# Expert loop of an attention and mixture-of-experts kernel: the high halves turned by transposing transfers, the low halves turned by TensorE as 2-byte blocks, 71 tiles instead of 72

## The reference

```
def _L0_ffn_ref(x, gate_w, expert_w):
    scores = jnp.einsum('bsh,eh->bse', x, gate_w)
    chosen = jnp.argmax(scores, axis=-1)
    onehot = jax.nn.one_hot(chosen, gate_w.shape[0], dtype=x.dtype)
    expert_out = jnp.einsum('bsh,efh->bsef', x, expert_w)
    return x + jnp.einsum('bsef,bse->bsf', expert_out, onehot)
x = x + _L0_xattn_ref(_layernorm(x, axis=-1), ctx_512, ctx_512, ...)
x = x + _L0_ffn_ref(_layernorm(x, axis=-1), L0_ffn_gate_w, L0_ffn_expert_w)
```

## Time and profile before

| | us |
|---|---|
| median of three runs | 975.7 |
| the profiled execution | 974.3 |
| its span, first to last instruction | 972.2 |
| PE busy in the span | 905.9 |
| DVE busy | 779.4 |
| POOL busy | 530.6 |
| ACT busy | 556.4 |
| PE, DVE, ACT and POOL busy between 760 and 960 us | 200.0, 119.0, 39.4, 145.4 |

### The profile page before, as it was taken

The page is one execution under the profiler, slowest core; times in us unless marked ns, Lnnn a source line. Parts: engine busy times, 40 slices in busy tenths (PEclk is TensorE's granted clock), DMA queues, the critical chain, the costliest instruction groups (busy, mean ns, idle before and its releaser), DMA issues. The chain is left out here.

```text
span 972.2 us, 27544 instructions
## 1 busy us (share of the span) xinstructions
PE 905.9 (93%) x8838; PEld 546.2 (56%) x8839; DVE 779.4 (80%) x1812; ACT 556.4 (57%) x928; POOL 530.6 (55%) x565
## 2 busy tenths in 40 slices
PE   5999999999899999899999999999775999999995
PEld 3446666556565665566556566566643555555552
DVE  8997999989699998879999889887793555555553
ACT  4686867768578686676867768657631111111110
POOL 2425454654546546455564554635552777777774
PEclk9998999999999999999999999998887999999998
DMA  9323142443424425233342542229233555555550
GB/s 316 98 69 108 39 138 75 135 124 75 134 62 138 120 72 150 68 122 102 97 143 59 146 106 65 78 67 327 77 131 98 169 170 172 163 167 167 174 174 21
DMA packets 81447, 119.51 MB, mean 123 GB/s; under 512 B 20465, under 2 KB 45797, under 8 KB 81327
## 3 DMA queue, kind: packets, MB, share of 16 engines
q1 hardware_dynamic: 68207, 81.63, 31.1%
q0 software_dynamic: 12048, 36.28, 9.9%
q10 hardware_dynamic: 1072, 0.02, 0.1%
HBM read 55.24 MB, written 38.13 MB: 96 GB/s over the span
## 5 line engine op out<-in xcount | busy, mean ns | idle before, releaser
L535 POOL TENSOR_TENSOR p_lo<-pf,p_hi 77x512 f16<-77x512 f32 x128 | 148.1, 1162 | 210.5 <-ACT p_hi L1128 210.2
L1127 ACT ACTIVATE pf<-scoresT,exp_scale 77x512 f32<-77x512 f32 x256 | 174.4, 681 | 73.2 <-PE scoresT L860 60.7
L1630 PE MATMUL mo<-e_w,x2T_hi 128*128 x576 | 184.5, 382 | 0.7 <-DVE x2T_lo L1667 0.7
L1128 ACT ACTIVATE p_hi<-scoresT,exp_scale 77x512 f16<-77x512 f32 x256 | 174.8, 683 | 0.0
L1650 ACT ACTIVATE x2T_hi<-mt 128x512 f16<-128x512 f32 x72 | 43.0, 597 | 183.4 <-PE mt L1619 183.4
L1677 DVE SCALAR_TENSOR_TENSOR res<-mo,inv,row 128x512 f32<-128x512 f32 x72 | 54.1, 751 | 91.6 <-PE mo L1630 91.6
L535 DVE TENSOR_TENSOR p_lo<-pf,p_hi 77x512 f16<-77x512 f32 x128 | 103.2, 822 | 14.8 <-ACT p_hi L1128 13.4
L1215 DVE TENSOR_REDUCE negmax<-work 128x4 f32<-128x308 f32 x256 | 112.6, 468 | 0.3 <-PE work L912 0.3
L1630 PE MATMUL mo<-e_w,x2T_lo 128*128 x288 | 110.1, 382 | 0.0
L1601 POOL DMA_INDIRECT out<-res,row x72 | 71.5, 993 | 65.4 <-DVE xn L1662 57.1
L832 PE MATMUL work<-wo_hi,cT_hi 128*128 128x512 f16 x256 | 97.3, 380 | 0.7 <-DVE cT_lo L1193 0.6
(11 more groups left out here) (257 smaller groups left out, 2179.5 us busy)
## 6 DMA issues: line engine op xcount, KB each, us to landing
row<-rows_by_expert SPq DMA_DIRECT2D x72, 257.5 KB, 3.0
q_st<-q_hi SPq DMA_DIRECT2D x256, 64.0 KB, 2.0
xt<-in_x SPq DMA_DIRECT2D x15, 1024.0 KB, 7.4
q_st<-q_lo SPq DMA_DIRECT2D x128, 64.0 KB, 2.0
ebuf<-in_L_ffn_expert_w SPq DMA_DIRECT2D x14, 512.0 KB, 8.3
er<-in_L_ffn_expert_w SPq DMA_DIRECT2D x7, 1024.0 KB, 14.9
out<-res,row POOLq DMA_INDIRECT x72, 2.8
xt<-in_x SPq DMA_DIRECT2D x4, 256.0 KB, 6.2
```

The costliest lines, as they stand in the source:

```text
L535: return tt.tensor_tensor(pp[1][0:LK, g % 2, j, :], pf[:, j, :], pp[0][0:LK, g % 2, j, :], ALU.subtract)
L1127: nc.scalar.activation(pf[:, j, :], sbank[n % SB][0:LK, :], ACT.Exp, scale=exp_scale[0:LK, :])
L1128: nc.scalar.activation(pp[0][0:LK, g % 2, j, :], sbank[n % SB][0:LK, :], ACT.Exp, scale=exp_scale[0:LK, :]).then_inc(sem("exp_done"), 1)
L1630: ins = nc.tensor.matmul(obank2[u % 2][:, :], x2T[ia][:, u % 2, k, :], w, start=k == 0 and n == 0, stop=k == KT - 1 and n == 2)
```

## The change

It touches the expert loop alone, and the number of tiles.

- `NTILE` is 71. The experts' rows fill at most 64 + 7 whole tiles, since 8192 is a multiple of 128 and eight roundings up then add less than eight tiles. The code of the loop is now eight tiles written out, seven turns of eight, and seven tiles written out.
- The split comes before the turning. ACT makes the high half `x2[0]` straight from the row buffer (`hi`, L1674: row x factor + offset, rounded to 2 bytes), three tiles ahead. DVE makes the low half `x2[1]` as `xn2` minus the high half, two tiles ahead (`lo`, L1710), and `norm` goes three tiles ahead (L1704).
- The high half is turned by a DMA issued by SP (L1592, `transpose=True`): 128 x 512 2-byte numbers, from on-chip memory to on-chip memory, four buffers (`TB`), three tiles ahead.
- The low half is turned by TensorE: four 128x128 transposes of 2-byte data against a 2-byte identity, `ident_h`, into a 2-byte PSUM tile; ACT copies it out (`lo`, L1682), in the place of its rounding of the high half.
- SP's queue holds in a tile's turn t: wait for `x2_hi` of t+3, transposing transfer of t+3, wait for the scatter of t-3 (`LAG`), load of t+5 into that scatter's buffer.
- `hi` waits until the matmuls of the tile four before it are done; `mm` waits for the transposing transfer of its tile; POOL's `add` also waits for `x2_hi`. The matmuls and the scatter are the same.

```diff
-NTILE = NTOK // P + E
+NTILE = NTOK // P + E - 1
+TB = 4
+LAG = 3
...
-            with sp.Fori(1, NTILE // U) as k:
-                for u in range(U):
-
-                    sp.wait_ge(sem(f"out{u}"), 16 * k)
-                    load_rows(sp, k * U + u, u)
+            def transpose(t, u):
+
+                wait_alone(sp, "x2_hi", t + 1)
+                sp.dma_start(x2T_hi[:, u % TB, :, :], x2[0][:, u % TB, :], transpose=True)\
+                    .then_inc(sem(f"x2T_in{u % TB}"), 16)
+
+            def body(t, k, u):
+                if has(t + TB - 1):
+                    transpose(t + TB - 1, (u + TB - 1) % U)
+                if isinstance(t, int) and t < LAG:
+                    return
+                if not has(t - LAG + U):
+                    return
+                v = (u - LAG) % U
+                wait_alone(sp, f"out{v}", 16 * (k + (u - LAG) // U + 1))
+                load_rows(sp, t - LAG + U, v)
+
+            for t in range(TB - 1):
+                transpose(t, t)
+            tiles(sp, body)
...
             def tr(t, u):
-                pe.wait_ge(sem("xn2_ready"), t + 1)
+                pe.wait_ge(sem("x2_lo"), t + 1)
                 pe.wait_ge(sem("t_used"), t + 1)
                 for k in range(KT):
-                    ins = nc.tensor.transpose(tbank[u % 2][:, k * P:(k + 1) * P], xn2[:, u, k * P:(k + 1) * P],
-                                              ident[:])
+                    ins = nc.tensor.transpose(tbank[u % 2][:, k * P:(k + 1) * P], x2[1][:, u % TB, k * P:(k + 1) * P],
+                                              ident_h[:])
...
-            def mm(t, u):
+            def mm(t, k8, u):
                 e = pe.value_load(tab[0:1, 1, bass.ds(t, 1)], min_val=0, max_val=E - 1)
+                pe.wait_ge(sem(f"x2T_in{u % TB}"), 16 * (k8 * (U // TB) + u // TB + 1))
                 pe.wait_ge(sem("t_used"), t + 1 + 2)
...
+            def hi(t, loads, u):
+                act.wait_ge(sem(f"row_in{u}"), 16 * loads)
+
+                act.wait_ge(sem("o_filled"), t + 1 + 2)
+                nc.scalar.activation(x2[0][:, u % TB, :], row[:, u, 0:DM], ACT.Identity,
+                                     scale=row[:, u, C_RSTD:C_RSTD + 1], bias=row[:, u, C_NMR:C_NMR + 1])\
+                    .then_inc(sem("x2_hi"), 1)
+
+            def lo(t, u):
+                act.wait_ge(sem("t_filled"), t + 1)
+
+                act.wait_ge(sem("o_filled"), t + 1 + TB)
+                nc.scalar.activation(x2T_lo[:, u % 2, :, :], tbank[u % 2][:, :].rearrange("p (k n) -> p k n", k=KT),
+                                     ACT.Copy).then_inc(sem("t_used"), 1)
...
             def lo(t, u):
-                dve.wait_ge(sem("t_hi"), t + 1)
-                nc.vector.tensor_tensor(x2T[1][:, u % 2, :, :], tbank[u % 2][:, :].rearrange("p (k n) -> p k n", k=KT),
-                                        x2T[0][:, u % 2, :, :], ALU.subtract).then_inc(sem("t_used"), 1)
+                dve.wait_ge(sem("x2_hi"), t + 1)
+                dve.wait_ge(sem("xn2_ready"), t + 1)
+                nc.vector.tensor_tensor(x2[1][:, u % TB, :], xn2[:, u, :], x2[0][:, u % TB, :], ALU.subtract)\
+                    .then_inc(sem("x2_lo"), 1)
```

More of the change, by code:

```diff
@@ L266, in build @@
     ident = sb("ident", [P, P])
+    ident_h = sb("ident_h", [P, P], F16)
     base = sb("base", [P, E])
@@ L1560, in build @@
         xn2 = at("xn2", [P, U, DM], F32, "q_st", 16384)
-        x2T = [at(f"x2T_{s}", [P, 2, KT, P], F16, "pf", n * 2048) for n, s in enumerate(("hi", "lo"))]
+        x2 = [at(f"x2_{s}", [P, TB, DM], F16, "pf", n * 4096) for n, s in enumerate(("hi", "lo"))]
+        x2T_hi = at("x2T_hi", [P, TB, KT, P], F16, "xt3")
+        x2T_lo = at("x2T_lo", [P, 2, KT, P], F16, "xt3", 4096)
         res = at("res", [P, U, DM], F32, "pp")
-        tbank = [st.enter_context(nc.psum_tensor(f"mt{i}", [P, 512], F32)) for i in range(2)]
+        tbank = [st.enter_context(nc.psum_tensor(f"mt{i}", [P, 512], F16)) for i in range(2)]
         obank2 = [st.enter_context(nc.psum_tensor(f"mo{i}", [P, 512], F32)) for i in range(2)]
         blk = st.enter_context(nc.Block())
-        assert NTILE % U == 0
+        assert 0 < NTILE % U and U % TB == 0
         def tiles(eng, body):
-            with eng.Fori(0, NTILE // U - 1) as k:
+            for u in range(U):
+                body(u, 0, u)
+            with eng.Fori(1, NTILE // U) as k:
                 for u in range(U):
                     body(k * U + u, k, u)
-            for u in range(U):
-                body(NTILE - U + u, NTILE // U - 1, u)
+            for u in range(NTILE % U):
+                body(NTILE - NTILE % U + u, NTILE // U, u)
         def has(t):
@@ L1592, in add @@
                 wait_alone(pool, "xn2_ready", t + 1)
+                pool.wait_ge(sem("x2_hi"), t + 1)
                 nc.gpsimd.tensor_tensor(row[:, u, 0:DM], row[:, u, 0:DM], xn2[:, u, :], ALU.add)\
@@ L1627, in mm @@
                 for k in range(KT):
-                    for n, (ia, ib) in enumerate(HL):
+                    for n, (turned, ib) in enumerate(((x2T_hi[:, u % TB, k, :], 0), (x2T_lo[:, u % 2, k, :], 0),
+                                                      (x2T_hi[:, u % TB, k, :], 1))):
                         w = e_w[:, bass.ds(e, 1), ib, k, :].rearrange("p a n -> p (a n)")
-                        ins = nc.tensor.matmul(obank2[u % 2][:, :], x2T[ia][:, u % 2, k, :], w,
+                        ins = nc.tensor.matmul(obank2[u % 2][:, :], turned, w,
                                                start=k == 0 and n == 0, stop=k == KT - 1 and n == 2)
@@ L1636, in body @@
                     tr(t + 1, (u + 1) % U)
-                mm(t, u)
+                mm(t, k, u)
+            pe.wait_ge(sem("ident_h_ready"), 1)
             tr(0, 0)
@@ L1643, in _ @@
         def _(act):
-            act.nop().then_inc(sem("o_filled"), 2)
-            def body(t, k, u):
[L1647 to L1651, removed]
+            act.nop().then_inc(sem("o_filled"), 2 + TB)
+            def hi(t, loads, u):
[9 more added lines that the diff above has]
+                                     ACT.Copy).then_inc(sem("t_used"), 1)
+            def body(t, k, u):
+                if has(t + 1):
+                    lo(t + 1, (u + 1) % U)
+                if has(t + TB - 1):
+                    hi(t + TB - 1, k + (u + TB - 1) // U + 1, (u + TB - 1) % U)
+            for t in range(TB - 1):
+                hi(t, 1, t)
+            lo(0, 0)
             tiles(act, body)
@@ L1658, in _ @@
             dve.nop().then_inc(sem("res_ready"), 2)
+            nc.vector.tensor_copy(ident_h[:], ident[:]).then_inc(sem("ident_h_ready"), 1)
             def norm(t, loads, u):
@@ L1665, in lo @@
             def lo(t, u):
-                dve.wait_ge(sem("t_hi"), t + 1)
-                nc.vector.tensor_tensor(x2T[1][:, u % 2, :, :], tbank[u % 2][:, :].rearrange("p (k n) -> p k n", k=KT),
-                                        x2T[0][:, u % 2, :, :], ALU.subtract).then_inc(sem("t_used"), 1)
+                dve.wait_ge(sem("x2_hi"), t + 1)
+                dve.wait_ge(sem("xn2_ready"), t + 1)
+                nc.vector.tensor_tensor(x2[1][:, u % TB, :], xn2[:, u, :], x2[0][:, u % TB, :], ALU.subtract)\
+                    .then_inc(sem("x2_lo"), 1)
             def body(t, k, u):
+                if has(t + 3):
+                    norm(t + 3, k + (u + 3) // U + 1, (u + 3) % U)
                 if has(t + 2):
[L1672 to L1675, removed]
+                    lo(t + 2, (u + 2) % U)
+                dve.wait_ge(sem("o_filled"), t + 1 + 2 + TB)
                 dve.wait_ge(sem("sum_ready"), t + 1)
@@ L1679, in body @@
                     .then_inc(sem("res_ready"), 1)
-            norm(0, 1, 0)
-            norm(1, 1, 1)
-            lo(0, 0)
+            for t in range(3):
+                norm(t, 1, t)
+            for t in range(2):
+                lo(t, t)
             tiles(dve, body)
```

3 lines of the change are left out of this document (1 added, 2 removed).

## The result

The changed kernel takes 1003.3 us (four runs, 1001.3 to 1015.3) against 976.3 us for the kernel before: ratio 1.0303, 95% interval 1.0261 to 1.0345. It is 27 us slower, where 967 us was predicted and 995 us was the end of the range. The profiled execution has a span of 999.5 us against 972.2. The ratios leave out two executions that took more than twice the usual time, one of the run "Load first" (2237 us) and one of the kernel before (3081 us).

A forecast was written before the change was run, and what follows sets the result against it. PE bounds the kernel before; afterwards SP's waits do. Changed loop 8 x 2.81 + 63 x 2.95 + 0.6 = 208.9 us against 217.9, so 975.7 - 9.0 = 966.7 us, about 967; range 956 to 995.

The forecast's parts named there:

- What bounds the kernel before: Expert loop: PE is never idle, 3.026 us a tile, while all other engines have slack.
- the floor: PE's shortest time for a tile in the changed loop: matmuls 2.59 plus transposes 0.22, 2.81 us.
- The new chain: Waits through SP's queue in the expert loop, claimed to set 2.95 us a tile.
- the circle: High half, SP's transposing transfer, load of t+5, its landing, next high half: 5.90 us for two tiles.
- T: How long the transposing transfer holds SP's queue: taken as 1.2 us, between 0.33 and 1.33.
- L: Landing of a row load after SP issues it: 3.0 us plus 0.15 behind the transposing transfer.
- SP's own reading: SP's scatter wait and start row before the load's issue, with a hand-over: 0.85 us.
- The first eight tiles: Start of the expert loop: buffers filled beforehand were to carry these tiles at 2.81 us each.
- The start: From DVE's first norm to the first matmul: 3.8 us against 3.3 now; 0.6 us added.
- Rival B: SP's queue held until the transposing transfer is nearly through, 2.0 us: 3.28 us a tile, 987 us; chance 0.25.
- Rival A: SP's hold by the transposing transfer is short, 0.33 us; PE stays the bound, 958 us; chance 0.24.
- Rival D: A tile's four transposed blocks land one behind the other, at most 8.0 us; loop 568 us; chance 0.04.

The follow-up runs named there:

- Load first: Changed kernel, but within a tile's turn SP issues the load of t+5 ahead of the transposing transfer of t+3; 974.9 us, ratio 0.9971.
- lag four: Changed kernel with LAG = 4 instead of 3, so the load of t+4 stands behind the transposing transfer of t+3; 1179.9 us.
- lag two: Changed kernel with LAG = 2 instead of 3, so the load of t+6 stands behind the transposing transfer of t+3; 974.7 us, ratio 0.9976.

## Why the prediction was wrong

- What bounds the kernel before: right as far as it went. The array was busy all the time, and the transposes' 0.44 us became 0.22. What I missed lay one step behind: PE's own sequencer needs 2.98 us a tile, so with the code as it is the floor was not 2.81. Even with an ideal transfer the gain in the loop would have been 0.04 us a tile, 2.8 us in all, beside the 3.0 of the tile saved, and not the 18.4 of the prediction. The rows of PE's sequencer were there to be read in the trace of before, and I read only its matmuls.
- The new chain: the circle was the right one, and it decided the time. Its size was not: 6.86 us instead of 5.90. The step that failed is the sum of the circle, 5.90 us, and in it the small terms read from a quiet kernel and the waits put at nothing. T and L, the unknown and the large one, were off by 0.05 and -0.25. The error of 1.2 us is in what I took for settled: the high half 0.81 and not 0.60 (its form was in no row); 0.52 and not 0.05 of waiting on ACT behind the low half, which waits for PE; the start of the transposing transfer, 0.18 and not 0.05; and SP's own reading, 1.20 and not 0.85, since the start row's read, 0.27 us at the median before, took 0.52. The bare circle at lag four is 6.25 us, so even without any queueing the sum was 0.35 short. The rest grew in the stops, and there DVE, held beside POOL, has a part that the prediction did not reckon with: it took DVE at 2.1 us a tile at most as having cover.
- Because of that, 0.475 us times 62 tiles, 29.5 us, is most of the miss of 36.6 us. The first eight tiles missed 3 us more: the buffers filled before the loop did not carry them at 2.81, since DVE's norm of a tile three ahead stands before the low half that PE needs next, and the first late landing stopped PE in tile 5. The start missed another 1.9 us (2.5 instead of 0.6). The sequencer's limit lay hidden below.
- Rival B forecast slower, by a longer hold of SP. Its number (T = 2.0) did not happen; T was 1.25. The point from which it decides, 3.09 us a tile, is near what the runs show (3.07 a tile took 978.7 us), and was passed by the other terms. I had put the upper end half way to 1003 us on the ground that T would have to be long; the circle as a whole should have been given that width.
- Rival A (short hold) is wrong by T. Rival D is wrong by the landing: by the semaphore records a whole transfer lands after a median of 2.4 us at lag four and 3.4 us in the changed kernel. The Trainium skill gives 1309 ns for a block (VectorE: DVE Perf Modes, The three transpose paths); the traces do not agree with four times that. By its rule that transposing transfers are as fast as ordinary ones (Advanced Engine Details and Errata, X-Bar Transpose (TRN2)) 128 KB should land in an estimated 2.0 to 3.0 us; the 2.4 us at lag four, where the DMA engines were busy 0.41 of the time, agree, and the 3.4 us in the changed kernel (0.72), against 2.7 for the 257.5 KB loads beside it, do not. It cost nothing: on average 5.0 us lay between this landing and the matmuls.
- By their busy time DVE and POOL were not the bound, as predicted. But DVE's norm rose from 0.54 to 0.73 us on average, and where it stood on PE's path that mattered; the prediction had not priced it (below).

## What to carry to other kernels

When a change puts a transfer into a queue ahead of loads, draw the circle of waits that closes through that queue and count how many tiles it has to close in; that whole number is worth more than any of its terms, and moving the load by one tile gave 29 us. Read the terms of such a circle with their queueing, since the waits in each engine's order are as real as the durations. And see whether a mean pace is even: here most of the loss lay in ten stops, and nearly every one held an instruction of DVE stopped beside POOL. Before shortening an engine's work, read its sequencer's rows: the time given back ends where the sequencer's own instructions begin.

## What the runs showed of the hardware

- A transposing transfer of 2-byte data inside on-chip memory holds SP's queue 1.23 us (median) for 128x512 and 1.13 for 128x128: almost nothing of it goes by size.
- PE's sequencer gave out some 41 instructions in 1.91 us, an estimated 0.047 us each (lag two); loading a register from memory with its check and the waits behind it took 1.07 us in the same tile.
- SP's read of one number from on-chip memory took 0.27 us at the median in the kernel before, 0.28 with a quarter of the transposing traffic, 0.52 in the changed kernel, and 0.34 with the high half first on ACT, at the full traffic. So it varies, and traffic alone does not order it.
- DVE's norm and low half can be stopped by POOL's addition. In the loop of the changed kernel 18 norms took over 0.7 us. Eleven of them had begun while an addition ran, the other seven while POOL issued the scatter ahead of it, and all ended some 0.3 us after the addition. The scatter's issue alone does not hold DVE: instructions that began and ended within it took their usual time. One case of a low half (DVE, then POOL):

```profile
864.07 2.26 DVE L1710 TENSOR_TENSOR x_lo<-xn,x_hi 128x512 f16<-128x512 f32 x1
```

```profile
863.48 0.99 POOL L1624 DMA_INDIRECT out<-res,row  x1 [0.41 <-issue]
864.48 1.29 POOL L1616 TENSOR_TENSOR row<-row,xn 128x512 f32<-128x512 f32 x1
```

  It normally takes 0.68 us; here it ended at 866.33, 0.56 us after POOL's addition (865.77). In the kernel before, 62 of 72 norms also began during an addition, but near its end, and none was longer than 0.57 us. The Trainium skill (SBUF — State Buffer, SBUF: two separate sides) describes a pair of ports that GpSimd shares with those VectorE instructions that have two inputs in that memory or run in a two-port mode, and that whichever starts first holds for its whole instruction. The trace agrees in that DVE waited out whole additions. It does not in who goes first: by the profile's start times the low half above, and nine instructions in all, began before the addition that they had to wait out. Whether the norm, with one such input, runs in a two-port mode no row shows.
